# Graph layer kernel: normalised rows turned by transposing DMAs through DRAM instead of on TensorE

## The reference

```python
Wh = h @ W.T                                   # 4096 x 256
norms = norm(Wh, axis=1)
sim = Wh @ Wh.T / (norms * norms.T + EPS)      # 4096 x 4096
alpha = softmax(where(adj > 0 or i == j, sim, -inf), axis=1)
x1 = layernorm(x + alpha @ Wh)
# second layer: mean over neighbours, three linear maps, relu, residual, layernorm
```

## Time and profile before

| what | us |
|---|---|
| time, median of 3 runs (lowest, highest) | 935.72 (935.14, 935.97) |
| profiled execution: span from first to last instruction | 932.6 |
| left around the span, against the median | 3.1 |
| TensorE busy in the span | 905.0 (97%) |
| VectorE, ScalarE busy | 607.4, 418.3 |

### The profile page before, as it was taken

One profiled execution on the slowest core, in us unless ns is written; L12 is line 12 of the kernel. 1 busy time (PEld: TensorE's weight loads), 2 busy tenths in 40 slices (PEclk: granted clock), 3 DMA queues, 4 the chain that ended last, 5 costly groups with the idle time before them and its releaser, 6 DMA issues.

```text
span 932.6 us, 21584 instructions
## 1 busy us (share of the span) xinstructions
PE 905.0 (97%) x7231; PEld 721.2 (77%) x7231; DVE 607.4 (65%) x1262; ACT 418.3 (45%) x701; POOL 65.5 (7%) x175
## 2 busy tenths in 40 slices
PE   7989999999999999999999999989899999999996
PEld 6857777777777777777777777668678888888885
DVE  2787786978767886688778788898443333333333
ACT  4955655656556655656656565550111011111110
POOL 2300000000000000000000000002110000000000
PEclk9999999999999999999999999999999999999998
DMA  8245554555545555565565575533131330330300
GB/s 260 69 158 160 153 155 143 148 158 149 161 142 159 173 155 159 140 189 145 164 186 143 164 256 163 165 117 131 68 131 38 118 125 29 118 124 24 122 28 17
DMA packets 113346, 126.03 MB, mean 135 GB/s; under 512 B 39105, under 2 KB 90594, under 8 KB 112130
## 3 DMA queue, kind: packets, MB, share of 16 engines
q1 hardware_dynamic: 113202, 125.10, 44.6%
q0 software_dynamic: 80, 0.13, 0.1%
HBM read 100.03 MB, written 25.18 MB: 134 GB/s over the span
## 4 chain that ended last, share of the span: by engine, by line
issue 88%; PE 5%; POOL 5%; DVE 1%; POOLq 1%; DMA 0%; ACT 0%; DVEq 0%; SPq 0%
PE ps L975 3%; POOL rstd L481 3%; POOL var_eps L479 1%; PE ps L987 1%; DMA feat_lo<-xT 0%; PE ps L1021 0%; DVE work L747 0%; POOLq L480 0%; ACT prob_hi L546 0%; DVE work L637 0%; POOLq L478 0%; DVE feat_hi L680 0%; DVE big L629 0%; DVE mix_extremes L706 0%; POOLq L483 0%
## 5 line engine op out<-in xcount | busy, mean ns | idle before, releaser
L1070 PE MATMUL ps<-feat_hi,prob_hi 128*128 128x257 f16 (+1 forms) x1024 | 279.8, 273 | 0.0
L1072 PE MATMUL ps<-feat_hi,prob_lo 128*128 128x257 f16 (+1 forms) x1024 | 279.4, 273 | 0.0
L1071 PE MATMUL ps<-feat_lo,prob_hi 128*128 128x256 f16 (+1 forms) x1024 | 278.9, 272 | 0.0
L1166 PE MATMUL ps<-big,mgroup 128*128 128x257 f16 x1024 | 227.9, 273 | 1.5 <-DVE big L819 1.5
L1167 PE MATMUL ps<-big,mgroup 128*128 128x256 f16 x1024 | 227.8, 273 | 0.0
L763 DVE SCALAR_TENSOR_TENSOR prob_lo<-work,prob_hi 128x512 f16<-128x512 f32 x256 | 175.9, 687 | 76.3 <-ACT prob_hi L546 73.8
L546 ACT ACTIVATE prob_hi<-work 128x512 f16<-128x512 f32 x256 | 154.6, 625 | 88.4 <-DVE work L756 48.7
L540 ACT ACTIVATE work<-ps 128x512 f32<-128x512 f32 x144 | 84.9, 592 | 142.4 <-PE ps L1008 124.9
L551 ACT ACTIVATE mask<-work 128x1024 fp8e4<-128x1024 f32 x128 | 133.6, 1043 | 0.0
L747 DVE SCALAR_TENSOR_TENSOR work<-adj_sb,work 128x512 f32<-128x512 int32 x144 | 99.2, 689 | 34.2 <-ACT work L540 29.1
L1071 PEld LDWEIGHTS ps<-feat_lo,prob_hi 128*128 128x128 f16 x1024 | 100.3, 98 | 27.2
(11 more groups left out here) (112 smaller groups left out, 825.0 us busy)
## 6 DMA issues: line engine op xcount, KB each, us to landing
adj_sb<-adjT SPq DMA_DIRECT2D x128, 512.0 KB, 3.9
mask_spill<-mask SPq DMA_DIRECT2D x128, 128.0 KB, 2.8
mgroup<-mask_spill SPq DMA_DIRECT2D x8, 2048.0 KB, 8.3
feat_lo<-xT SPq DMA_DIRECT2D x8, 512.0 KB, 5.5
xres<-x SPq DMA_DIRECT2D x8, 512.0 KB, 5.5
x_spill<-rows SPq DMA_DIRECT2D x8, 512.0 KB, 4.6
xres<-x_spill SPq DMA_DIRECT2D x32, 128.0 KB, 2.4
out<-rows SPq DMA_DIRECT2D x32, 128.0 KB, 1.7
```

Source lines behind the costliest of these rows:

```text
L1070: pe.matmul(acc(D + 1), prob_hi[:, s, cols], feat_hi[:, jb, 0:D + 1], start=start, stop=False)
L1071: pe.matmul(acc(D), prob_hi[:, s, cols], feat_lo[:, jb, :], start=False, stop=False)
L1072: return pe.matmul(acc(D + 1), prob_lo[:, s, cols], feat_hi[:, jb, 0:D + 1], start=False, stop=stop)
L1166: pe.matmul(agg_ps(q, D + 1), lhsT, x1_hi_of(jb // GB)[:, jb % GB, 0:D + 1], start=(jb == 0), stop=False)
```

## The change

The eight `turn_units` leave TensorE, and with them the 16 copies out of PSUM. SP does a new `turn_units(g)`: it waits for both halves of the group, stores them to the DRAM scratch `unit_spill` (two slots), waits until that has landed, and issues two transposing DMAs from the scratch into the group's columns of `unitT_hi` and `unitT_lo`. The engines that waited for the turned copies now wait for the landing of these DMAs (`unitT_loaded`, one semaphore for even and one for odd groups). The 16-bit identity matrix and its two GpSimd instructions go too.

```diff
+    unit_spill = nc.dram_tensor("unit_spill", [2, 2, GW, D], F16, kind="Internal").ap()
...
+            def turn_units(g):
+                sync.wait_ge(unit_ready, g + 1)
+                sync.dma_start(unit_spill[g % 2].rearrange("h (b p) d -> p h b d", p=P),
+                               unit[:, g % 2]).then_inc(unit_stored[g % 2], 16)
+                sync.wait_ge(unit_stored[g % 2], 16 * (g // 2 + 1))
+                for half, to in enumerate((unitT_hi, unitT_lo)):
+                    sync.dma_start_transpose(to[:, :, g * GW:(g + 1) * GW],
+                                             unit_spill[g % 2, half]).then_inc(unitT_loaded[g % 2], 16)
+
             for g in range(4, G):
                 sync.wait_ge(wh_done, g - 3)
                 load_xT(g)
+                if g > 4:
+                    turn_units(g - 5)
             load_unit(0, 1, 0, 2)
             load_unit(0, 1, 1, 3)
+            for g in range(3, G):
+                turn_units(g)
...
             def unit_heads(g):
                 act.wait_ge(norm_ready, g + 1)
-                wait(act, unitT_done, g - 1)
+                wait(act, unitT_loaded[g % 2], UNIT_TURNED * (g // 2))
...
             split_features(0)
-            unitT_out(G - 2)
+            dve.wait_ge(unitT_loaded[0], UNIT_TURNED * (G // 2))
...
                     if a == 0 and j == 0:
-                        unitT_out(G - 1)
+                        dve.wait_ge(unitT_loaded[1], UNIT_TURNED * (G // 2))
...
-            for g in range(4):
+            for g in range(G):
                 project(g)
-            for g in range(G - 4):
-                turn_units(g)
-                project(g + 4)
-            turn_units(G - 4)
...
-            pe.wait_ge(unitT_hi_ready, 1)
-            pe.wait_ge(unitT_lo_ready, 1)
+            pe.wait_ge(unitT_loaded[0], UNIT_TURNED)
             direct_scores(0, 0, 0, 0)
...
-            pe.wait_ge(unitT_hi_ready, G)
-            pe.wait_ge(unitT_lo_ready, G)
+            for i in range(2):
+                pe.wait_ge(unitT_loaded[i], UNIT_TURNED * (G // 2))
```

More of the change, by code:

```diff
@@ L150, in gnn_program @@
         ident = sb("ident", [P, P], F32)
-        ident16 = sb("ident16", [P, P], F16)
         ones = sb("ones", [P, P], F32)
@@ L195, in wh_ps @@
             return ps[:, 2 * slot + b // 2, (b % 2) * D:(b % 2 + 1) * D]
-        def unitT_ps(slot, half):
-            return ps[:, 4 + 2 * half + slot, :].bitcast(F16).rearrange("p (k i) -> p k i", k=KD)
         def score_ps(tile):
@@ L234, in gnn_program @@
         unit_ready = sem("unit_ready")
-        unitT_done = sem("unitT_done")
-        unitT_hi_ready = sem("unitT_hi_ready")
-        unitT_lo_ready = sem("unitT_lo_ready")
+        unit_stored = [sem(f"unit_stored{i}") for i in range(2)]
+        unitT_loaded = [sem(f"unitT_loaded{i}") for i in range(2)]
         bias_wide_ready = sem("bias_wide_ready")
@@ L295, in gnn_program @@
         PHASE0_POOL = G * 3
+        UNIT_TURNED = 16 * 2
         @block.sync
@@ L442, in _ @@
             pool.memset(ident[:, :], 0.0).then_inc(consts_cleared, 1)
-            pool.memset(ident16[:, :], 0.0).then_inc(consts_cleared, 1)
             pool.memset(ones[:, :], 1.0).then_inc(ones_ready, 1)
@@ L448, in _ @@
             pool.memset(minus_half[:, :], -0.5).then_inc(ones_ready, 1)
[L449 to L452, removed]
+            pool.wait_ge(consts_cleared, 1)
+            pool.affine_select(out=ident[:, :], in_=ident[:, :], compare_op=ALU.not_equal, fill=1.0, base=0,
+                               pattern=[[-1, P]], channel_multiplier=1).then_inc(consts_ready, 1)
             pool.wait_ge(ones_ready, 2)
@@ L496, in squares @@
                 ins.then_inc(nsq_ready, 1)
-            def unitT_out(g):
-                act.wait_ge(unitT_done, g + 1)
-                act.activation(unitT_hi[:, :, g * GW:(g + 1) * GW], unitT_ps(g % 2, 0), ACT.Copy).then_inc(unitT_hi_ready, 1)
             def unit_heads(g):
                 act.wait_ge(norm_ready, g + 1)
-                wait(act, unitT_done, g - 1)
+                wait(act, unitT_loaded[g % 2], UNIT_TURNED * (g // 2))
                 for b in range(GB):
@@ L528, in _ @@
                     setup_out(1, mixw[:, KD:2 * KD, :].rearrange("p k n -> p (k n)"), 1, KD * D)
-                unitT_out(g - 1)
             act.wait_ge(flag_ready, 1)
@@ L556, in diagonal @@
                 exponentials(t0, f0, 0, STEP_TILES)
-                if a == 0:
-                    unitT_out(G - 1)
                 for j in range(GB):
@@ L640, in unit_tails @@
                 ins.then_inc(unit_ready, 1)
-            def unitT_out(g):
-                dve.wait_ge(unitT_done, g + 1)
-                dve.tensor_copy(unitT_lo[:, :, g * GW:(g + 1) * GW], unitT_ps(g % 2, 1)).then_inc(unitT_lo_ready, 1)
             chain = Steps(dve, dve_step, 0)
@@ L655, in _ @@
                     widen_biases()
-                if 0 < g < G - 1:
-                    unitT_out(g - 1)
             dve.wait_ge(norm_ready, G)
@@ L977, in project @@
                 ins.then_inc(wh_done, 1)
[L979 to L989, removed]
             pe.wait_ge(w0_loaded, 16)
-            pe.wait_ge(consts_ready, 2)
-            for g in range(4):
+            pe.wait_ge(consts_ready, 1)
+            for g in range(G):
                 project(g)
-            for g in range(G - 4):
-                turn_units(g)
-                project(g + 4)
-            turn_units(G - 4)
             def direct_scores(a, jb, t, j):
@@ L1026, in _ @@
             combine(0, w_selfT_sb, 3)
-            turn_units(G - 3)
             combine(1, w_nbT_sb, 1)
-            turn_units(G - 2)
             pe.wait_ge(extremes_ready, 1)
@@ L1042, in _ @@
             direct_scores(0, 1, 1, 1)
-            turn_units(G - 1)
             pe.wait_ge(bias_wide_ready, 1)
```

## The result

The changed kernel takes 966.19 us (median of 4 runs, 964.35 to 966.99), the kernel before in the same session 935.43 us (934.21 to 935.97): a ratio of 1.033 with a 95% interval of 1.0313 to 1.0346, slower by 31 us. The forecast was 981.1 us, in a range of 948 to 1085.

The account below looks back on a forecast made before the run. TensorE's work was taken to bound the kernel, with stage 1 waiting for both tables. Tables at 21.6 + 8 x 8.6 + 1.4 + 6.0 = 97.8 us: 932.6 + 42.3 + 3.1 restart + 3.1 span to median = 981.1 us, range 948 to 1085.

Parts of the forecast that it names:

- Direction and mechanism: SP's serial store, wait and turn chain completes the tables late, delaying the third tile's scores by 42.3 us; slower, chance 0.97.
- Store, S = 4.6: 512 KB store to the scratch on SP: 4.6 us from issue to landing, taken from the x_spill store; lower bound 2.8.
- Turning DMA, X = 2.0: Each 256 KB transposing DMA from the scratch: 2.0 us, twice the plain price; bounds 1.0 and 96 us.
- the SP issues lie beside them: In SP's queue, issues of 0.38 us each were taken to run beside the transposes' data, adding nothing to 8.6 us a turn.
- stores 8 to 10 us apart: Sign expected in the new trace: unit_spill stores on SP 8 to 10 us apart after the fourth.
- Transfers between, 6.0 us: Two xT and two adjacency loads issued between the first four turns: 512 KB each, 1.5 us each, 6.0 us in all.
- fixed part: Part of a load's landing independent of its bytes, put at 1.4 us and added once as the last landing.
- Restart, 3.1: TensorE's first matmuls after its long idle time run slower, as at the program's start; 3.1 us, counted once.
- The slots: Two slots of unit: two turns of one slot cost 13.7 us, less than SP's 17.2, so SP binds.
- The moved steps: Late xT loads, norm extremes, scales, adjacency loads, norm row and broadcast moved behind turns; last projection ends near 46 us, covered.
- The two rules: Skill pages on transposing DMAs: as fast as regular ones gives 965.1 us; 1309 ns a block, assuming no overlap, gives 1117 us.

Follow-up runs that it names:

- experiment 5: On top of experiment 2, SP issues each group's store ahead of the previous group's turning DMAs, with loads moved; 945.37 us, ratio 1.0119 to the kernel before.
- experiment 2: Changed kernel with eight scratch slots, and unit_heads waiting for the store alone instead of the turned landing; 966.05 us, ratio 1.032 to the kernel before.
- experiment 4: Changed kernel plus ten useless matmuls on TensorE just before it waits for the last turned half; 963.78 us, ratio 1.0304 to the kernel before.
- experiment 3: On top of experiment 2, plain loads of the same bytes replace the sixteen transposing DMAs, so rows arrive unturned; 959.08 us, ratio 1.0259 to the kernel before.
- experiment 6: On top of experiment 5, plain loads of the same bytes replace the transposing DMAs; 939.54 us, ratio 1.006 to the kernel before.
- experiment 10: All stores issued first, turns after, against a kernel with early stage 1, earlier adjacency loads and four unit slots; 936.30 us, ratio 1.0018 to the kernel before.

## Why the prediction was right, and which terms were mis-sized

**Direction and mechanism: right.** The tables were complete late, stage 1 was released by a DMA into `unitT_lo`, and the rest took as long as before. The cause is SP's serial order, store, wait, turn: changing that order alone, the loads' place in it included (experiment 5 against experiment 2), gives back 19 to 21 of the 31 us, while changing only the slots gives nothing. The size was missed: the forecast loss was 45.4 us, the measured one 30.8.

**Store, S = 4.6: too long.** It lands 3.6 us after its issue in the late turns, and 3.2 the first time. The row of `x_spill` was the wrong neighbour: it takes 4.7 us after the change, too. It lies in stage 1 among the adjacency loads and mask stores; that these make it slower is not shown.

**Turning DMA, X = 2.0: too long, and the wrong kind of cost.** I priced data, and took SP's issue for 0.38 us as in plain rows. Measured, the issue is 1.28 us, and the next store lands 3.6 us after its own issue although the turned data are ahead of it: a turn is 3.6 + 2 x 1.28 = 6.2 us and not 8.6. This is the step that failed: "the SP issues lie beside them" was the other way about. The prediction's own sign of being wrong, "if SP is held while issuing one", came true, and its stores 8 to 10 us apart were 6.2. Over eight turns it is 19.2 us too much together with S.

**Transfers between, 6.0 us: too short.** The three early gaps are 10.1, 9.9 and 10.7 us against 6.2, so 12.1 us together. I counted the data of the loads alone. Their issues are 0.6 us of a gap and 1.1 of the third; most of the rest is the store behind them, which lands 2.9 and 3.0 us later behind one `xT` load and 3.4 us later behind two adjacency loads. Why one load costs nearly as much as two is open.

Both together: 97.8 - 19.2 + 6.1 and a remainder of 0.5 give the measured 85.2 us. The remainder fits a slip in the working: by the step of 0.5 us for each 128 KB, the 2.4 us of a 128 KB load leave a fixed part of 1.9 us, not 1.4. The sum was 12.6 us too late, and would have been 18.7 too late if the short gaps had not offset a third of the long turns; that much is luck. The 12.6 us are most of the error of 15 us in the time; 1.1 us are the restart, less 0.8 us by which the rest of the program was longer, and 2.1 us that the new median lies only 1.0 us above the profiled span, not 3.1, in part because now the slowest execution is the profiled one.

**Restart, 3.1: measured 2.0 us.** The granted clock does show it here, as it did not at the program's start, and experiment 4 ties it to what TensorE does before the scores.

**The slots: right, but closer than forecast.** VectorE's last tail of group 6 ends at 69.79 and its store is issued at 70.60, so 0.8 us of slack where the forecast had 3.5. **The moved steps: right.** The projection of group 7 was late (43.2 to 49.5 us, where the forecast ended it near 46; it took 6.3 us at the lower clock, not 3.7), and covered.

**The two rules.** The two halves land after 3.6 and 3.4 us, and the plain loads of the same bytes in experiment 3 after 3.0 and 3.2. That is near the Trainium skill's rule that turning DMAs are as fast as regular ones (Advanced Engine Details and Errata, X-Bar Transpose (TRN2)); experiment 6 shows that it is not quite so, by 1.2 us of all DMA engines a group. By its 965.1 us the forecast would have been almost exact, though by an error in two terms of opposite sign. The estimate of 10.5 us for a half, eight times the 1309 ns that the Trainium skill gives for one block (VectorE: DVE Perf Modes, The three transpose paths), does not hold: a half lands within 3.7 us of its issue in the changed kernel, and where only turning DMAs follow each other one is issued every 1.3 us (experiment 5, 57.13 to 59.82 us). So the blocks of one DMA overlap; the estimate assumed that they don't.

## What to carry to other kernels

A transfer that goes out and comes back is priced by its order of issue, not by its bytes: wait for a store only after the next store and the previous turn are issued, if the slots allow it. When the order is mended, look at the DMA share again, since the next bound may be there and no order helps against it. Work taken from TensorE wins nothing while the path that replaces it is the one that releases TensorE; with the best order found here the DMA path only drew level (935.81 us, ratio 1.0011).

## What the runs showed of the hardware

A turning DMA of 256 KB holds SP for 1.24 to 1.30 us in the late turns of the changed kernel, against 0.5 to 0.6 for a plain one of the same bytes in experiment 3. Behind other transfers it holds SP longer: 2.0 to 2.2 us behind a store of 512 KB and 5.16 us behind two adjacency loads and a store (experiment 5), 5.66 us for the second one behind the 2 MB broadcast (experiment 10). The length of an issue on SP thus tells how much stands ahead of it in the queue. Where only turning DMAs of 256 KB follow each other, one is issued every 1.3 us, and a group of 512 KB stored and 512 KB turned keeps the DMA engines full for 4.1 us (share 1.19 to 1.22, experiment 5).
